# Two more sequences of layer 1 through routed experts, in a two-layer transformer on one core

## The chip, the cores and the metric

The kernel runs on one core of a Trainium2 chip. The metric is the device time of one execution in microseconds. Of the kernel before there are three timed runs and one profiled execution.

## What is computed

Eight sequences of 512 tokens, 128 wide, go through two layers. Each layer is adaptive layer norm, attention with 16 heads of 8, adaptive layer norm again, and a mixture of 8 experts of which each token uses two. Layer 0 has full attention, SwiGLU experts of hidden width 352 and a shared expert; layer 1 has low-rank q, k and v, causal attention and experts with a squared relu. What the change touches is the expert part of layer 1:

```python
def _L1_ffn_ref(x, Wr, W1, W2):           # N = 8 * 512 tokens, E = 8, D = F = 128
    probs = softmax(xf @ Wr)
    w, idx = top_k(probs, 2)
    comb = zeros((N, E)).at[arange(N)[:, None], idx].add(w)
    mid = square(maximum(einsum('nd,edf->enf', xf, W1), 0.0))
    y = einsum('enf,efd->end', mid, W2)
    return einsum('end,ne->nd', y, comb)
```

## The kernel before

The 8 sequences of layer 0 are numbered 0 to 7, the same ones in layer 1 are 8 to 15. The work of a sequence i is cut into steps with names, each on one engine:

- p_*: layer norm (statistics on VectorE, its power on GpSimd, normalisation on ScalarE, a turn on TensorE), projections, and the split of q and k into three bf16 parts that are stored in HBM; "stack" loads them back (tiles QS, KS). "c_ks" writes ones into rows of KS that only the second pass of the scores reads.
- score, rowmax: scores on TensorE and their row maxima on VectorE (line 965), 32 of each; the maxima make a round trip through HBM (max_st, max_ld). Then bscore, expo (ScalarE, line 1320) and pv (line 775).
- u_*, t_*: sums and outputs through HBM and back, division, output projection, residual.
- f_*: layer norm, transposed activations hF, router logits (f_lg, line 1016), top two (f_top, f_idx).

**Two ways through the experts.** A sequence that stands in GROUPS is routed, the others are dense.

*Dense* (`if i not in GROUP`, sequences 10 to 15): all 8 experts on all 512 tokens. For each expert d_up (TensorE, line 873, weights r1), d_relu and d_sq (ScalarE, lines 1395, 1404), d_dn (TensorE, line 880, weights r2), d_y (VectorE times the token's weight, lines 1216, 1223), d_add (GpSimd adds, line 1549); then d_x (lines 1555, 1558) and d_out, the store of the result. Sequences 14 and 15 have four buffers for relu and square, two of which lie in the weight buffers wst of the routed experts; sequence 15 adds up on VectorE.

*Routed* (groups of two sequences, q = 0 to 4): r_hx makes the activations token by token (GpSimd), r_keep keeps the choices, and the rr_* steps (VectorE, lines 1080 to 1151, and two matmuls) count tokens by expert and give each token a place in tiles of 128 that belong to one expert each. r_sc (GpSimd, line 1504) scatters 8 tiles of tokens twice to d_h by indirect DMA. A group has MT = 23 tiles. In layer 1 they go by fours (index L): x_ld loads, x_turn turns (line 828), x_w loads each tile's expert weights by a register, x_up (line 847), relu, square, x_dn (line 865), x_y, and x_st stores to d_y. g_ga (GpSimd, line 1528) gathers 8 tiles twice, g_w weights and adds them (VectorE, lines 1176, 1180), g_x (GpSimd, lines 1536, 1542) adds them into X. In layer 1 the result is then stored.

A scatter waits until the scatter of the tile before in the same half has landed, a gather likewise. The second source tile of the scatters is `r2[:, 0:NT, :]`, so the load of the dense weights r2 (line 264) is put behind the last scatter of the last group.

**What sets the order.** A planner, run when the kernel is built, gives every engine and the SP queue one fixed list. Each step has a weight (its assumed time), a due time ("urgency"), steps it comes after and a lag. Where several steps can start within SLACK of each other on an engine, the one with the smallest due time is put first. The tables SHIFT, LATE, LAST and NUDGE add offsets to due times; NUDGE has one offset for each family and sequence. Waits on semaphores follow from the data; an engine works through its list in order.

## Time and profile before

| | |
|---|---|
| median of three runs | 1128.35 us (1123.76 to 1128.52) |
| profiled execution | 1132.48 us, of which the span is 1130.3 us |
| TensorE matmul busy | 1026.9 us (91%) |
| VectorE busy | 869.8 us (77%) |
| ScalarE busy | 730.9 us (65%) |
| GpSimd busy | 429.5 us (38%) |
| mean granted TensorE clock | 0.949 of full speed |

The page gives busy times over the span, the chain of work that ended last (followed back from the last instruction, at each step to what released it), and the costliest groups of instructions. "x" is a count of instructions; a float32 matmul stands as two passes in the trace, so it counts twice. DVE is VectorE, ACT ScalarE, POOL GpSimd, SP the engine whose queue issues most DMAs. The idle time before an instruction is put down to what ended it.

### The profile page before, as it was taken

To read this page: it belongs to the slowest core of one execution; us is meant where nothing else is said; L and a number is where in the kernel's file an instruction comes from. 1 tells how busy PE (TensorE), PEld (TensorE's weight loads), DVE (VectorE), ACT (ScalarE), POOL (GpSimd) and SP (SyncE) were. 2 spreads that over 40 slices of the span, in tenths; PEclk is the share of its full clock that TensorE was granted. 3 is DMA by queue.
4 is the path that set the end of the run, shared out by engine and by line. 5 is a ranking of instruction groups with operands and counts; after the bars stand their busy time and mean duration, and the time that the engine had idled before them with its cause. 6 is when DMAs were issued, how large, how long until landed. Compare 5 with 4: busy or idle time off the path is not lost.

```text
span 1130.3 us, 22735 instructions
## 1 busy us (share of the span) xinstructions
PE 1026.9 (91%) x8315; PEld 533.1 (47%) x8315; DVE 869.8 (77%) x1814; ACT 730.9 (65%) x1220; POOL 429.5 (38%) x484
## 2 busy tenths in 40 slices
PE   4589999889989999899889999899999889999996
PEld 2112222224555555446555566566565434455464
DVE  3799888898887888797557877777876688687455
ACT  4048766877767776666466566565657767767763
POOL 3000212354033346325135433453344468434463
PEclk9569988999999999999898999999999999999998
DMA  4804434356664777557548577695767846412110
GB/s 136 173 24 129 112 87 114 112 189 180 214 203 149 235 205 215 155 161 201 152 139 230 155 226 232 192 249 179 229 185 220 222 126 183 104 43 61 50 40 19
DMA packets 122510, 176.06 MB, mean 156 GB/s; under 512 B 20280, under 2 KB 86200, under 8 KB 122400
## 3 DMA queue, kind: packets, MB, share of 16 engines
q1 hardware_dynamic: 116064, 161.24, 49.1%
q0 software_dynamic: 5760, 12.59, 3.9%
q8 instruction: 66, 1.08, 0.4%
q10 hardware_dynamic: 576, 0.79, 0.3%
q14 instruction: 44, 0.36, 0.1%
HBM read 114.77 MB, written 59.67 MB: 154 GB/s over the span
## 4 chain that ended last, share of the span: by engine, by line
PE 46%; DVE 20%; DMA 15%; issue 8%; ACT 4%; POOL 3%; SPq 3%; POOLq 0%; DVEq 0%; ACTq 0%
DVE nm L965 12%; PE ps L775 10%; PE ps L837 8%; PE ps L758 5%; PE ps L736 5%; PE ps L856 5%; DMA gr<-d_y,pos 4%; PE ps L873 2%; PE ps L880 2%; DMA DR<-d_r 2%; ACT ES L1320 2%; DMA d_h<-r,pos 2%; PE ps L785 2%; DMA d_r<-DC 1%; PE ps L718 1%
## 5 line engine op out<-in xcount | busy, mean ns | idle before, releaser
L965 DVE TENSOR_REDUCE nm<-ps 128x2 f32<-128x1024 f32 (+3 forms) x512 | 507.7, 1016 | 103.5 <-PE ps L742 57.2
L1320 ACT ACTIVATE ES<-ps 128x1024 f32<-128x1024 f32 (+3 forms) x512 | 430.0, 862 | 160.3 <-PE ps L758 90.1
L775 PE MATMUL ps<-ES,VS 128*9 128x512 f32 (+3 forms) x2048 | 231.1, 528 | 0.8 <-DVE nmp L976 0.4
L736 PE MATMUL ps<-KS,QS 48*128 48x512 bf16 (+3 forms) x1024 | 183.8, 366 | 38.5 <-DVE nm L965 23.6
L758 PE MATMUL ps<-QS,KS 51*128 51x512 bf16 (+3 forms) x1024 | 178.0, 352 | 20.0 <-DVE nm L965 11.6
L837 PE MATMUL ps<-hsT,wst 128*128 128x128 f32 x1104 | 158.6, 288 | 3.7 <-DVE hdx L1158 3.4
L837 PEld LDWEIGHTS ps<-hsT,wst 128*128 128x128 f32 x1104 | 136.9, 194 | 38.6 <-issue 30.1
L758 PEld LDWEIGHTS ps<-QS,KS 51*128 51x128 bf16 x1024 | 49.6, 94 | 173.7 <-DVE nm L965 55.2
L736 PEld LDWEIGHTS ps<-KS,QS 48*128 48x128 bf16 x1024 | 50.0, 95 | 153.6 <-DVE nm L965 59.3
L1528 POOL DMA_INDIRECT gr<-d_y,pos x80 | 83.2, 1040 | 99.4 <-DMA gr<-d_y,pos 63.5
L856 PE MATMUL ps<-wst,hdx 128*128 128x128 f32 x552 | 84.7, 291 | 0.6 <-ACT hsT L1347 0.4
L856 PEld LDWEIGHTS ps<-wst,hdx 128*128 128x128 f32 x552 | 71.4, 197 | 21.5 <-issue 13.2
L1504 POOL DMA_INDIRECT d_h<-hx,pos x40 | 40.0, 999 | 103.5 <-DVE pos L1135 57.7
L1549 POOL TENSOR_TENSOR ya<-ya,yS 128x512 f32<-128x512 f32 x35 | 45.1, 1290 | 73.3 <-DVE yS L1223 73.3
L1456 POOL TENSOR_SCALAR rs<-mv 128x4 f32<-128x4 f32 x32 | 7.5, 236 | 168.2 <-DVE mv L951 167.6
L1158 DVE SCALAR_TENSOR_TENSOR hdx<-tx,ps 128x384 f32<-128x384 f32 x92 | 50.4, 548 | 22.5 <-ACT tx L1353 22.0
L1353 ACT ACTIVATE tx<-ps 128x384 f32<-128x384 f32 x92 | 45.3, 492 | 34.0 <-PE ps L837 32.2
L1259 ACT ACTIVATE xn<-X,rs 128x128 f32<-128x128 f32 x128 | 52.5, 485 | 18.6 <-POOL rs L1461 18.6
L775 PEld LDWEIGHTS ps<-ES,VS 128*9 128x9 f32 x2048 | 31.8, 89 | 68.2 <-issue 53.6
L1465 POOL TENSOR_TENSOR sp<-sr,sp 128x512 bf16<-128x512 f32 x32 | 37.3, 1171 | 56.7 <-ACT sp L1296 56.5
L1165 DVE TENSOR_TENSOR hdx<-ps,hdx 128x384 f32<-128x384 f32 x92 | 50.7, 551 | 9.1 <-PE ps L837 8.2
L742 PE MATMUL ps<-codek,codeq 64*128 64x128 bf16 x512 | 56.3, 219 | 0.0
(196 smaller groups left out, 1405.4 us busy)
## 6 DMA issues: line engine op xcount, KB each, us to landing
wst<-we SPq DMA_DIRECT2D x92, 576.0 KB, 5.1
d_u<-US SPq DMA_DIRECT2D x64, 256.0 KB, 2.7
KS<-d_k SPq DMA_DIRECT2D x64, 192.0 KB, 4.8
QS<-d_q SPq DMA_DIRECT2D x64, 192.0 KB, 5.5
hs<-d_h SPq DMA_DIRECT2D x25, 256.0 KB, 4.0
d_y<-ys SPq DMA_DIRECT2D x25, 256.0 KB, 4.7
d_q<-sp SPq DMA_DIRECT2D x16, 384.0 KB
d_k<-sp SPq DMA_DIRECT2D x16, 384.0 KB, 3.4
```

The source lines that it names most:

```text
L736: mm = eng.matmul(psum[:, bank[u][a], 0:n], QS[m][r:r + KA, pr, 128 * t:128 * t + 128], KS[m][r:r + KA, pr, 0:n], start=True, stop=i < NB)
L742: mm = eng.matmul(psum[:, bank[u][a], n - 128:n], codeq[r:r + 64, :], codek[r:r + 64, :], start=False, stop=True)
L758: mm = eng.matmul(psum[:, bank[u][a], 0:S - q0], KS[m][r:r + KB, pr, 128 * j:128 * j + 128], QS[m][r:r + KB, pr, q0:S], start=True, stop=i ...
L775: mm = eng.matmul(psum[32 * a:32 * a + 9, b, q0:S], VS[i % 3][:, j, 4 * g + a, :], ES[(2 * (NT * (NG * i + g) + j) + a // 2) % NES][:, a % ...
L837: mm = eng.matmul(ps(*u)[:, 128 * n:128 * n + 128], w[:, c, 128 * n:128 * n + 128], hsT[m][:, a0:a0 + 128], start=True, stop=True)
L856: mm = eng.matmul(ps(*u)[:, 0:128], hdx[UNIT[p, j] % 2][:, 128 * n:128 * n + 128], w[:, 2, 128 * n:128 * n + 128], start=(n == 0), stop=(n ...
L965: eng.tensor_reduce(nm[f][:, :].rearrange("p (a c) -> p a c", a=2)[:, :, 4 * pr + t], ps2("score", i, f, pr, t)[:, :, 0:n], AX.X, ALU.max, ...
L1158: eng.scalar_tensor_tensor(out=hdx[m][:, :], in0=tx[m][:, :], scalar=1.0, in1=ps("x_up", p, j, 0)[:, 0:384], op0=ALU.add, op1=ALU.mult).th ...
L1165: eng.tensor_tensor(hdx[m][:, :], ps("x_up", p, j, 1)[:, 0:384], hdx[m][:, :], ALU.mult).then_inc(s[k], 1)
L1259: ins = eng.activation(xn[w][:, t, :], X[:, NT * b + t, :], ACT.Identity, bias=rs[:, w, 2, t:t + 1], scale=rs[:, w, 1, t:t + 1])
L1320: eng.activation(ES[(2 * n + pp) % NES][:, :, 0:S - q0], ps2("bscore", i, f, g, j, pp)[:, :, 0:S - q0], ACT.Exp, scale=SC1 if i >= NB else ...
L1528: eng.indirect_dma_start(out=gr[m][:, :], out_offset=None, in_=d_y[p][:, :], in_offset=bass.IndirectOffsetOnAxis(ap=pos[p % 2][:, c, t8:t8 ...
```

## The change

Sequences 10 and 11 become a sixth group of GROUPS, so they are routed, and only 12 to 15 are dense. Everything sized by GROUPS follows: the group's own indirect DMAs, tiles and waits, r2's load behind the scatters of (10, 2), the dense buffers of sequence 14 behind the last expert of (10, 2). The load of the ones into KS (c_ks) comes after the second stack of sequence 0 in the plan. The assumed times of three counting steps depend on the size of the group; for two sequences they become 0.96, 3.6 and 0.96 us instead of 1.25, 3.8 and 1.2. SLACK goes from 0.05 to 0.15, and all 13 rows of NUDGE are new, by up to some 6 units for the families u, t, g and d.

```diff
--- before.py
+++ after.py
@@ -22,7 +22,7 @@
 
 NST = 4
 
-GROUPS = ((0, 2), (2, 2), (4, 2), (6, 2), (8, 2))
+GROUPS = ((0, 2), (2, 2), (4, 2), (6, 2), (8, 2), (10, 2))
 GMAX = max(n for _, n in GROUPS)
 
 MT = [2 * n * NT + E - 1 for _, n in GROUPS]
@@ -78,19 +78,19 @@
 
 
 NUDGE = {
-    "p": [-0.65, 2.4, 0.46, -0.17, -0.01, 0.52, -0.35, -0.35, -0.36, 0.0, 0.0, 0.0, 0.01, -0.04, 0.06, -0.44],
-    "score": [0.1, 0.0, 0.0, 0.0, 0.0, 0.0, 0.0, 0.0, 0.0, 0.0, 0.0, 0.0, -0.02, 0.03, 0.11, 0.1],
-    "max": [-0.03, 0.04, -0.27, -0.13, -0.32, -0.1, -1.24, -0.14, 0.0, 0.01, 0.0, -0.04, -0.01, 0.28, 0.07, 1.6],
-    "expo": [0.0, 0.0, 0.0, 0.0, 0.0, 0.0, 0.0, 0.0, 0.0, 0.0, -0.04, 0.0, -0.08, -0.02, -0.07, -0.09],
-    "pv": [-0.02, 0.91, 0.27, -0.08, 0.02, -0.01, -0.02, 0.0, 0.0, 0.0, 0.02, -0.01, -0.03, -0.19, -0.25, 0.21],
-    "u": [0.51, -0.26, 0.32, -0.59, -0.7, -0.3, -0.77, -0.67, -0.29, 0.68, 0.99, 0.1, 1.49, 0.61, 0.88, -1.31],
-    "t": [-0.5, -0.89, -0.57, -1.24, -0.7, -1.24, -0.53, -0.05, 0.07, 0.0, 0.01, 0.46, -1.06, 0.77, -0.38, 1.37],
-    "f": [0.01, 0.01, -0.1, 0.01, 0.06, -0.01, 0.0, 0.11, -1.15, -1.33, 0.44, -0.55, -0.34, -1.93, -2.64, -3.12],
-    "s": [0.26, -0.18, 0.01, 0.17, 0.12, -0.09, 0.0, 0.0, 0.0, 0.0, 0.0, 0.0, 0.0, 0.0, 0.0, 0.0],
-    "r": [-0.74, -0.04, 0.02, 0.01, -0.35, -1.37, 0.25, 0.36, 0.45, 1.63, 0.0, 0.0, 0.0, 0.0, 0.0, 0.0],
-    "x": [0.0, 0.0, 0.0, 0.0, -0.64, 0.0, 0.0, 0.0, 0.0, 0.0, 0.0, 0.0, 0.0, 0.0, 0.0, 0.0],
-    "g": [0.52, 1.36, -0.05, 0.59, 0.12, 2.56, 1.49, 0.89, -0.68, 1.19, 0.0, 0.0, 0.0, 0.0, 0.0, 0.0],
-    "d": [0.0, 0.0, 0.0, 0.0, 0.0, 0.0, 0.0, 0.0, -0.48, -1.4, 0.4, 0.18, 0.59, 1.17, 1.02, 0.96],
+    "p": [1.01, 2.21, 0.34, 0.79, 0.04, 1.01, -0.36, -0.36, -0.36, 0.0, 0.0, 0.03, 0.01, -0.07, 0.66, 1.29],
+    "score": [0.09, 0.0, 0.0, 0.0, 0.0, 0.0, 0.0, 0.0, 0.0, 0.0, 0.09, 0.0, -0.05, -0.03, 0.13, 0.08],
+    "max": [-1.47, 0.05, 0.71, -0.45, -1.35, -0.67, -0.64, 0.2, -0.01, 0.08, 0.03, 0.01, 1.32, -1.86, -0.82, -0.21],
+    "expo": [0.0, 0.0, 0.0, 0.0, 0.01, 0.0, 0.0, 0.0, 0.0, 0.0, -0.04, 0.14, 0.06, 0.01, -0.02, 1.08],
+    "pv": [-0.15, 0.94, 0.22, -0.11, -0.01, -0.06, -0.09, -0.03, -0.05, 0.05, 0.07, 0.11, 0.6, 1.55, -0.18, 2.01],
+    "u": [-1.88, -2.81, -0.31, -4.63, -2.38, -5.63, -3.24, -4.06, -1.33, -3.46, -1.45, -1.52, -1.29, -5.93, -5.45, -4.69],
+    "t": [-1.62, -1.87, -0.87, 0.26, -3.41, -2.27, -0.07, 0.12, 0.02, -0.03, -0.35, -1.87, -0.14, 0.03, -0.97, 5.02],
+    "f": [0.17, -1.54, -2.64, 0.09, 0.05, -0.97, 0.05, 0.06, -2.37, -3.46, 0.17, -0.01, -0.59, -0.93, -2.03, -1.12],
+    "s": [0.26, -0.32, 0.02, -0.15, -0.08, -0.09, 0.01, 0.0, 0.0, 0.0, 0.0, 0.0, 0.0, 0.0, 0.0, 0.0],
+    "r": [-1.09, -0.39, -0.04, 0.08, -0.83, -1.16, 0.54, 3.47, 0.62, 0.59, 1.34, 2.9, 0.0, 0.0, 0.0, 0.0],
+    "x": [-0.1, 0.0, 0.0, 0.2, -0.77, 1.19, 0.0, 0.0, 0.0, 0.0, 0.0, 0.0, 0.0, 0.0, 0.0, 0.0],
+    "g": [1.2, 1.31, -1.38, 0.29, -1.94, 2.99, 3.21, 1.03, -5.02, 1.58, -0.45, 4.01, 0.0, 0.0, 0.0, 0.0],
+    "d": [0.0, 0.0, 0.0, 0.0, 0.0, 0.0, 0.0, 0.0, 0.52, -0.61, 0.0, 2.99, 0.34, 1.92, 1.64, 3.53],
 }
 TIED = {"stack": "p", "rowmax": "score", "bscore": "expo", "rr": "r"}
 
@@ -200,7 +200,7 @@
 
 PIPE = 1.3
 WEARLY = 0.2
-SLACK, SWITCH = 0.05, 0.1
+SLACK, SWITCH = 0.15, 0.1
 
 XAT, XLEN = (2.6, 1.6), (2.0, 1.6)
 SPREAD = 2.5, 2
@@ -245,7 +245,7 @@
     add("DVE", ("c_ps",), 3.4, -10.0)
     add("DVE", ("c_one",), 1.2, -1.0, [("m_one", 0)])
     for m in range(NSTK):
-        add("SP", ("c_ks", m), 0.8, 0.1 + 0.1 * m, [("c_one",)], lag=2.5)
+        add("SP", ("c_ks", m), 0.8, 0.1 + 0.1 * m, [("c_one",), ("stack", 0, 1)], lag=2.5)
 
     for b in range(2, NB):
         load(f"x{b}", b - 1.0, 5.0, after=[("stack", b - 1, 1)])
@@ -387,9 +387,9 @@
             u = i + 2.45
             add("DVE", ("rr_oh", q), 0.2, u, [("r_keep", first + c) for c in range(size)])
             add("PE", ("rr_mm", q), 0.4, u, [("rr_oh", q), ("c_more", 1)], opens=1)
-            add("DVE", ("rr_a", q), 1.25, u, [("rr_mm", q)], closes=[("rr_mm", q)])
-            add("DVE", ("rr_pos", q), 3.8, u, [("rr_a", q)] + ([("g_ga", GROUPS[q - 1][0] - 1, t, c) for t in range(NT) for c in range(2)] if q > 1 else []))
-            add("DVE", ("rr_tex", q), 1.2, u, [("rr_pos", q)] + ([("x_reg", q - 2, (MT[q - 2] - 1) // 12)] if q > 1 else []))
+            add("DVE", ("rr_a", q), 0.8 + 0.08 * size, u, [("rr_mm", q)], closes=[("rr_mm", q)])
+            add("DVE", ("rr_pos", q), 3.2 + 0.2 * size, u, [("rr_a", q)] + ([("g_ga", GROUPS[q - 1][0] - 1, t, c) for t in range(NT) for c in range(2)] if q > 1 else []))
+            add("DVE", ("rr_tex", q), 0.7 + 0.13 * size, u, [("rr_pos", q)] + ([("x_reg", q - 2, (MT[q - 2] - 1) // 12)] if q > 1 else []))
             sent = [("rr_pos", q)] * 4
             for t in range(size * NT):
                 for c in range(2):
```

## Rows read from the trace of the kernel before

**Rows 1.** The page's busy times: engine, busy us (share of the span), instructions.

```profile
PE 1026.9 (91%) x8315; PEld 533.1 (47%) x8315; DVE 869.8 (77%) x1814; ACT 730.9 (65%) x1220; POOL 429.5 (38%) x484
```

**Rows 2.** The page's chain that ended last, shares of the span by engine.

```profile
PE 46%; DVE 20%; DMA 15%; issue 8%; ACT 4%; POOL 3%; SPq 3%; POOLq 0%; DVEq 0%; ACTq 0%
```

**Rows 3.** By stretch: busy us (instructions) of PE, PEld, DVE, ACT, POOL; clock; DMA share; GB/s.

```profile
530.00:600.00 70.00, 62.14 (x460) 38.04 (x458) 40.13 (x91) 40.40 (x65) 24.36 (x25) 0.90 0.52 155
870.00:926.00 56.00, 48.14 (x539) 23.40 (x537) 40.22 (x75) 38.36 (x69) 30.72 (x31) 0.97 0.68 191
926.00:1072.00 146.00, 142.05 (x1411) 70.44 (x1407) 106.88 (x251) 109.23 (x193) 71.98 (x70) 1.00 0.33 89
957.00:1124.00 167.00, 158.58 (x1411) 87.53 (x1409) 113.97 (x283) 115.26 (x206) 75.09 (x72) 0.98 0.20 54
```

**Rows 4.** Listing of the dense up line: duration min/median/max, first and last start.

```profile
L873 PE MATMUL ps<-hF,r x80: 592/593/1061, 926.3 to 1102.3; 128*128 128x512 f32 x80
```

**Rows 5.** Groups by shape, TensorE: xcount | busy us, mean ns | idle before, releasers.

```profile
L880 PE MATMUL ps<-r,hd 128*128 128x128 f32 x320 | 44.4, 283 | 0.5 <-DVE sr L958 0.4
...
L873 PE MATMUL ps<-hF,r 128*128 128x512 f32 x80 | 43.9, 647 | 2.2 <-DVE ya L1216 2.2
...
L828 PE MATMUL ps<-ident,hs 128*128 128x128 f32 x115 | 19.2, 290 | 0.1
...
L865 PE MATMUL ps<-wst 128*128 128x128 f32 x46 | 6.7, 288 | 0.0
...
L847 PE MATMUL ps<-hsT,wst 128*128 128x128 f32 x46 | 6.6, 286 | 1.9 <-DMA wst<-wy 1.8
```

**Rows 6.** Groups by shape, ScalarE: the squares of the dense experts.

```profile
L1404 ACT ACTIVATE hd<-tt 128x512 f32<-128x512 f32 x40 | 25.0, 633 | 0.5
```

**Rows 7.** Groups by shape, VectorE, from 870 to 960 us.

```profile
L1180 DVE SCALAR_TENSOR_TENSOR cv<-gr,wts,cv 128x128 f32<-128x128 f32 x16 | 7.8, 489 | 2.6 <-DMA gr<-d_y,pos 2.1
...
L1223 DVE TENSOR_TENSOR yS<-ps,comb 128x512 f32<-128x512 f32 x4 | 2.7, 675 | 0.0
```

**Rows 8.** Groups by shape, GpSimd, whole span.

```profile
L1528 POOL DMA_INDIRECT gr<-d_y,pos x80 | 83.2, 1040 | 99.4 <-DMA gr<-d_y,pos 63.5 <-issue 29.2 <-DMA d_y<-ys 4.4
...
L1549 POOL TENSOR_TENSOR ya<-ya,yS 128x512 f32<-128x512 f32 x35 | 45.1, 1290 | 73.3 <-DVE yS L1223 73.3
...
L1504 POOL DMA_INDIRECT d_h<-hx,pos x40 | 40.0, 999 | 103.5 <-DVE pos L1135 57.7 <-DMA d_h<-hx,pos 38.9 <-issue 6.8
```

**Rows 9.** Timeline of VectorE: start us, us, instruction [idle before].

```profile
800.90 0.19 DVE L1016 TENSOR_TENSOR lg<-lg,sm 128x32 f32<-128x32 f32 x1
...
808.02 0.43 DVE L1080 TENSOR_TENSOR ohb<-ohs 128x64 bf16<-128x64 f32 x1
...
814.79 0.18 DVE L1151 TENSOR_SCALAR tex<-te 128x24 uint32<-128x24 f32 x1
...
944.88 0.19 DVE L1016 TENSOR_TENSOR lg<-lg,sm 128x32 f32<-128x32 f32 x1
```

**Rows 10.** Timeline of GpSimd: scatters, gathers and the last addition of group (8, 2).

```profile
813.80 1.14 POOL L1504 DMA_INDIRECT d_h<-hx,pos  x1 [11.36 <-DVE pos L1135]
...
847.84 0.97 POOL L1504 DMA_INDIRECT d_h<-r,pos  x1 [0.77 <-DMA d_h<-r,pos]
...
909.34 1.01 POOL L1528 DMA_INDIRECT gr<-d_y,pos  x1 [0.35 <-issue]
...
959.86 1.27 POOL L1542 TENSOR_TENSOR X<-X,cv 128x512 f32<-128x512 f32 x1
```

**Rows 11.** Timeline of SP's queue near the start.

```profile
11.35 5.68 SPq L1604 DMA_DIRECT2D KS<-wst  x8
```

**Rows 12.** The chain that ended last, its pieces near the start: start us, us, what.

```profile
16.97 1.53 ACT xn L1259 x4
...
56.06 16.98 DVE nm L965 x15
```

**Rows 13.** DMA issues: KB each, median us from issue to landing.

```profile
r<-wr SPq DMA_DIRECT2D x2, 512.0 KB, 3.9
```

## The prediction

> **What bounds the kernel now.** I read the page first: TensorE is busy for 1026.9 of 1130.3 us [rows 1], and it holds 46% of the chain that ended last, with VectorE at 20% and DMAs at 15% [rows 2]. A share that high over the whole span still hides stages, so the busy times by stretch come next [rows 3]. The reader should see three kinds. From 926 to 1072 us dense expert work of layer 1, whose first matmul starts at 926.3 [rows 4], lies beside attention: TensorE is busy for 142.05 of 146 us, 0.973. From 870 to 926 us no dense work exists yet, only attention and the routed end of sequences 6 to 9: 48.14 of 56 us, 0.86, and its granted clock slips to 0.97. From 530 to 600 us, around the change of layers, 62.14 of 70. So where dense work is on offer TensorE is the limit, and where it isn't TensorE waits for attention's round trips. Then the groups of instructions by engine gave prices [rows 5 to 8], and the timelines gave the latency of the one layer 1 group that is routed already, sequences 8 and 9 [rows 9, 10].
>
> **What goes and what comes on TensorE.** The dense block of a sequence is 8 products up (16 passes in the trace) and 32 down (64 passes). The five sequences 10 to 14 spend 43.9 and 44.4 us on them [rows 5], so one costs 8.8 + 8.9 = 17.7 us, and two that go save 35.3. In their place comes what group (8, 2) has: 23 tiles turned (19.2 us for the five groups, 3.8 for one), 23 up (46 passes, 6.6 us), 23 down (6.7 us), and two small counting matmuls; the dearest small matmul shown has a mean of 0.290 us, so 0.6 at most [rows 5]. That is 17.7 us. TensorE is relieved of 35.3 - 17.7 = 17.6 us.
>
> **The other engines.** ScalarE loses 16 relus and 16 squares, 32 x 0.633 = 20.3 us with the row of the squares for both, and gets four passes over 23 tiles, 5.75 full banks each, 23 x 0.633 = 14.6 us [rows 6]: 5.7 us less. VectorE loses 16 products at 0.675, 10.8 us, and gets 8 pairs of weighting at 0.489 each, 7.8 us, beside the counting chain, which fills 808.0 to 814.9 us for the present group between other work; some 4.6 us of it are its own, an estimate from 20 short instructions of 0.17 to 0.46 us. It comes out within 2 us of even [rows 7, 9]. GpSimd loses 14 additions at 1.29 and two closing pairs at 1.27 each half, 23.1 us, and gets 16 scatters at 1.0, 16 gathers at 1.04, and four full-tile pairs at 1.27 each half (two masks, two closings), 10.2 us: 42.8 us, so +20 us busy [rows 8, 10]. It has room: 75.09 of 167 us from 957 on [rows 3]. But it also stands still for its own transfers: before 80 gathers it was idle for 99.4 us, 1.24 each, so 16 take 36 us of its queue if nothing is put between them [rows 8].
>
> **When the new group can run.** Its router needs sequence 11, whose logits are ready at 944.88 us; for sequence 9 that was 800.90 [rows 9]. From 800.90 the present group needs 12.9 us to the first scatter (813.80), 34.0 more to the last one's issue (847.84), 61.5 to its first gather (909.34), and 51.8 to the end of its last addition into X (959.86 + 1.27): 160.2 us [rows 10]. Laid from 944.88: scatters 958 to 993, gathers from 1053, done at 1105, and some 5 us for the store of the result, an estimate a little above that load's time: 1110. The dense block of sequence 12 now has to wait as well. Its second weights (r2) share memory with the second scatter source and are loaded behind the last scatter, now 993 instead of 849; with the 3.9 us that such a load takes to land, 997 [rows 13]. The third and fourth buffers of sequences 14 and 15 come free with the group's last expert, about 1050; that costs nothing unless TensorE gets to the block of 14, the last but one, before then.
>
> **The sum.** From 926 to 997 us, 71 us, the dense work that filled TensorE is gone and nothing can take its place. I give this stretch the share of its neighbour before it, 0.86 for 0.973: 71 x 0.113 = 8.0 us of the saving stay unused [rows 3]. Attention's round trips (maxima out and back, sums out and back) are what ends last there. Behind 997 dense work of 12 to 15 (71 us) and the experts (17.7) fill it as now. Net 17.6 - 8.0 = 9.6 us: span 1130.3 - 9.6 = 1120.7. The routed chain's 1110 lies before that by 10 us. The profiled execution took 1132.48 (2.2 beside its span) and the median of the runs shown is 1128.35, 4.1 below, so 1128.35 - 9.6 = 1118.7, say 1118.5.
>
> **The small edits.** The ones for KS hold SP's queue from 11.35 to 17.03 us [rows 11] ahead of the first stores. Moved behind the first stacks they free it, but the chain there runs through ScalarE (normalisation of sequence 1, 16.97 to 18.50, ahead of the second part of the split) [rows 12], and the stack waits for the third part. Gain 0 to 1.6 us; I take 0. Behind the stacks the eight issues (5.7 us) stand before sequence 1's stores, whose scores come only after the maxima of sequence 0, the last of which end at 73.0 us [rows 12]: 0, or 5.7 us if that cover went. The smaller weights of the three counting steps, the slack and the offsets execute nothing; they change orders on all five queues over the whole span. The trace has no row for that. I bound it by the hole at 530 to 600: at 0.973 it would be 68.1 busy for 62.14, so 6 us to gain and, as a second hole like it, 6 to lose; I take 0 since no row leans either way.
>
> **A rule against this change.** Indirect DMAs are what the change adds on GpSimd. Over 80 scatters and 80 gathers the trace shows means of 1.0 and 1.04 us, beside a VectorE that is three quarters busy [rows 3, 8]. The Trainium skill, page "SBUF — State Buffer", section "SBUF: two separate sides", says that while VectorE copies or scales in its two-port mode GpSimd cannot write a transfer's descriptors, and that such a DMA of some 0.62 us alone took about 3.1. Estimated by that page, 32 new ones would hold GpSimd 99 us in place of 33, which would make it the limit. The trace doesn't show it, so it gets no chance beyond that of rival (b), whose price is made from rows and which it would bring about.
>
> **Rivals.** (a) *The saving is swallowed by the gap.* If dense work of 12 can't start at 997 (its logits or the order on the queues hold it) and TensorE runs at 0.86 over all 146 us from 926 to 1072, 146 x 0.113 = 16.5 us are lost, net 1.1: 1127. For it: the dense block is the only filler, and sequence 12's own attention must be through. Against: attention, freed of 35 us of competing matmuls, gets there sooner.
> (b) *GpSimd's queue puts the routed chain last: slower.* GpSimd works in order. The dense additions of 12, 13 and 14 (7 x 1.29 + 2 x 1.27 = 11.6 us each, 35) now share the time from 993 to 1105 with scatters, gathers and their waits. If all of them fall in series with the routed chain, it ends at 1110 + 35 = 1145, 14.7 us over the present span: 1143. For it: while the present group's scatters ran, no dense block had begun [rows 4, 10]. It decides from the point where more than 11 of the 35 us are in series (1120.7 - 1110); if 20 are, it is level with now. Against it: waits of 1.24 us before a gather can take an addition of 1.29.
> (c) *No gap at all.* Reordered attention fills TensorE without dense work: -17.6, and with the hole at 530 closed -23.6: 1110.8 to 1104.8. Against it: the routed chain's 1110 on the span's scale (1106 on the median's) is a floor unless sequence 11's logits come sooner.
> (d) *The offsets do the most,* in either direction, by up to 6 us and for reasons apart from the routing; it widens each case.
>
> **How the numbers follow.** Forecast, 1112 to 1122.7: 0.46. (c), below 1112: 0.13. (a) and weak forms of (b), within 0.5% (1122.7 to 1134): 0.23. (b) beyond: 0.18. Half a per cent is about what a measurement of this kernel can tell from no change. So faster 0.59, same 0.23, slower 0.18. Range 1105 to 1138: it takes in most of (c) and the nearer part of (b).
>
> **What would show it.** TensorE's busy time falls by 17 to 18 us; the share between 926 and the last scatter is about 0.86, with the granted clock slipping for moments; the last scatter is issued near 993 and dense matmuls down start just after it; the last addition of sequence 11 is 10 us or more before the end, with sequence 15's dense block last as now. Wrong: if scatters or gathers stand last in the chain (b); if TensorE's share stays at 0.86 past 1010 (a); if the time moved before 870 us (d).

## The result, with the profile after

The changed kernel is slower, by 1.2%. Its median is 1140.68 us (1134.48 to 1144.05, four runs) beside 1127.55 us for the kernel before on the same chip (1123.76 to 1128.52, four runs): a ratio of 1.0116 with an interval of 1.0067 to 1.0166. Measured again on two other chips the ratio was 1.0078 (1.0050 to 1.0105) and 1.0153 (1.0095 to 1.0211). The prediction said 1118.5 and a range of 1105 to 1138, so the time lies outside, on the side that was given 0.18. Five executions of all that follow stand out as slow and are left out of the ratios, though not of the medians: three of the kernel before, one of run 3, and one of run 10 (2602.78 us). The profiled execution took 1140.92 us with a span of 1139.1, 8.8 more than the span before.

The busy times of the page, changed kernel; they answer to [rows 1]:

```profile
PE 1028.0 (90%) x8272; PEld 532.0 (47%) x8272; DVE 880.2 (77%) x1832; ACT 726.7 (64%) x1212; POOL 450.8 (40%) x506
```

TensorE has 43 instructions fewer, and yet 1.1 us more busy time, where 17.6 less were forecast. The instructions themselves are not the cause. The groups of TensorE by shape, changed kernel (count, busy us, mean ns, idle before), stand against [rows 5]:

```profile
L873 PE MATMUL ps<-hF,r 128*128 128x512 f32 x48 | 28.1, 685 | 3.1 <-DVE ya L1216 2.2 <-DVE yS L1223 0.6 <-DVE lg L1016 0.2
L880 PE MATMUL ps<-r,hd 128*128 128x128 f32 x192 | 26.1, 280 | 2.8 <-DVE yT L995 1.7 <-DVE yS L1223 1.1
L828 PE MATMUL ps<-ident,hs 128*128 128x128 f32 x138 | 22.1, 281 | 0.7 <-DMA hs<-d_h 0.6
L865 PE MATMUL ps<-wst 128*128 128x128 f32 x92 | 14.4, 302 | 0.0
L847 PE MATMUL ps<-hsT,wst 128*128 128x128 f32 x92 | 13.2, 285 | 0.2 <-ACT ES L1320 0.2
```

The dense groups fall by 15.8 and 18.3 us, the three routed ones rise by 2.9, 7.7 and 6.6: 16.9 us net of the 17.6 worked out. All other matmuls together take 18.0 us more, with the same work. Where that happens is seen in the busy times by stretch, changed kernel, in the columns of [rows 3]:

```profile
530.00:600.00 70.00, 67.11 (x547) 40.90 (x545) 48.75 (x101) 47.23 (x75) 27.61 (x28) 0.98 0.64 187
870.00:926.00 56.00, 48.67 (x483) 24.61 (x481) 35.24 (x77) 36.64 (x66) 32.13 (x34) 0.88 0.55 160
926.00:1072.00 146.00, 131.87 (x1285) 64.27 (x1286) 100.05 (x243) 99.47 (x178) 82.57 (x83) 0.89 0.51 145
957.00:1124.00 167.00, 153.59 (x1356) 83.86 (x1351) 106.73 (x264) 111.60 (x202) 89.75 (x89) 0.94 0.37 106
...
926.00:1000.00 74.00, 62.81 (x621) 27.55 (x621) 56.57 (x150) 47.49 (x86) 47.70 (x49) 0.82 0.62 170
```

The same last stretch of the kernel before:

```profile
926.00:1000.00 74.00, 70.95 (x700) 34.77 (x696) 57.56 (x127) 56.55 (x100) 44.99 (x46) 1.00 0.50 128
```

From 926 to 1000 us TensorE's share is 62.81 / 74 = 0.849 for 0.959, and the granted clock has a mean of 0.82 of full speed for 1.00. The clock has two levels, 1.2 and 2.4 GHz, so 0.82 means 2 x 0.18 x 74 = 27 us at 1.2 GHz there, and 0.88 from 870 to 926 another 13: 40 us for 3.4 before. It fell while TensorE worked in pieces with waits between them. What that does to a matmul, in the groups by shape from 870 to 996 us, changed kernel first, then the kernel before:

```profile
L775 PE MATMUL ps<-ES,VS 128*9 128x512 f32 x80 | 13.5, 753 | 0.1
```

```profile
L775 PE MATMUL ps<-ES,VS 128*9 128x512 f32 x80 | 10.8, 610 | 0.2
```

The same 80 matmuls take a mean of 753 ns for 610. So the busy time that was saved came back as slower matmuls, 1.1 us more than was saved, and the idle time of TensorE grew from 103.4 to 111.1 us: 1.1 + 7.7 = 8.8, the growth of the span. This is how the account closes, not yet what the cause is.

The new group itself. GpSimd's timeline, changed kernel (start, us, instruction, idle before in brackets): first and last scatter, first gather, last addition into X.

```profile
948.53 1.16 POOL L1504 DMA_INDIRECT d_h<-hx,pos  x1 [1.93 <-DVE pos L1135]
...
984.18 0.98 POOL L1504 DMA_INDIRECT d_h<-r,pos  x1 [0.30 <-issue]
...
1034.73 1.17 POOL L1528 DMA_INDIRECT gr<-d_y,pos  x1 [7.85 <-issue]
...
1080.51 1.27 POOL L1542 TENSOR_TENSOR X<-X,cv 128x512 f32<-128x512 f32 x1
```

It is done at 1081.8, 57 us ahead of the end. Two listings of the changed kernel (duration min/median/max, first and last start) show when dense work begins, the first line answering to [rows 4]:

```profile
L873 PE MATMUL ps<-hF,r x48: 592/595/1220, 1031.8 to 1113.6; 128*128 128x512 f32 x48
```

```profile
L865 PE MATMUL ps<-wst x92: 275/275/581, 869.0 to 1030.9; 128*128 128x128 f32 x92
```

The first dense matmul starts at 1031.8, right behind the last product of the last routed expert at 1030.9, and not at 997.

Last, VectorE's timeline gives the moments at which a sequence's router logits are ready, here of sequences 11 to 15 in the changed kernel and then in the kernel before, whose first is the 944.88 of [rows 9]:

```profile
932.50 0.19 DVE L1016 TENSOR_TENSOR lg<-lg,sm 128x32 f32<-128x32 f32 x1
990.29 0.19 DVE L1016 TENSOR_TENSOR lg<-lg,sm 128x32 f32<-128x32 f32 x1
1032.43 0.19 DVE L1016 TENSOR_TENSOR lg<-lg,sm 128x32 f32<-128x32 f32 x1
1091.33 1.04 DVE L1016 TENSOR_TENSOR lg<-lg,sm 128x32 f32<-128x32 f32 x1
1113.70 0.19 DVE L1016 TENSOR_TENSOR lg<-lg,sm 128x32 f32<-128x32 f32 x1
```

```profile
1001.51 0.19 DVE L1016 TENSOR_TENSOR lg<-lg,sm 128x32 f32<-128x32 f32 x1
1048.05 0.19 DVE L1016 TENSOR_TENSOR lg<-lg,sm 128x32 f32<-128x32 f32 x1
1080.28 0.86 DVE L1016 TENSOR_TENSOR lg<-lg,sm 128x32 f32<-128x32 f32 x1
1102.46 0.19 DVE L1016 TENSOR_TENSOR lg<-lg,sm 128x32 f32<-128x32 f32 x1
```

Sequences 11, 12 and 13 are 12.4, 11.2 and 15.6 us ahead of before; sequences 14 and 15 are 11.1 and 11.2 behind. The lead is there and is lost between 13 and 14.

The traces narrow down where. The exponentials (expo, line 1320) go through the sequences one after another. Their listing for sequences 14 and 15 together (duration min/median/max, first and last start), changed kernel and then before:

```profile
L1320 ACT ACTIVATE ES<-ps x64: 366/712/1032, 976.3 to 1079.9; 128x1024 f32<-128x1024 f32 x16, 128x768 f32<-128x768 f32 x16, 128x512 f32<-128x512 f32 x16, 128x256 f32<-128x256 f32 x16
```

```profile
L1320 ACT ACTIVATE ES<-ps x64: 378/730/1032, 981.1 to 1072.1; 128x1024 f32<-128x1024 f32 x16, 128x768 f32<-128x768 f32 x16, 128x512 f32<-128x512 f32 x16, 128x256 f32<-128x256 f32 x16
```

The changed kernel begins them 4.8 us ahead and ends them 7.8 us behind: 103.6 us for 91.0. What follows lasts 59.2 us for 58.2, so nearly the whole growth of the span is there once they are through. Two more traces of the changed kernel have 104.9 and 100.0 us (runs 9 and 12 below). In this stretch, from 976 to 1080 us, stand the new group's expert products, 17.1 us of TensorE, and 14.1 us of its passes on ScalarE.

Sequence 14 is sequence 6 in layer 1 and can't start ahead of the routed result of 6 in layer 0. GpSimd's timeline, the addition that closes one half of it, changed kernel and then before:

```profile
896.42 1.27 POOL L1542 TENSOR_TENSOR X<-X,cv 128x512 f32<-128x512 f32 x1
```

```profile
893.72 1.27 POOL L1542 TENSOR_TENSOR X<-X,cv 128x512 f32<-128x512 f32 x1
```

That is 2.7 us later, in a kernel whose TensorE has been relieved of work that lay behind this point.

### The profile page after: what moved, and what is told of

It reads as the page before. It is cut to its first block, busy times and chain, and to the rows that moved or that the text cites. A ratio compares the mean times of both kernels' runs of the same rounds, so it can differ in the third digit from the quotient of the medians.

```text
span 1139.1 us, 22772 instructions
## 1 busy us (share of the span) xinstructions
PE 1028.0 (90%) x8272; PEld 532.0 (47%) x8272; DVE 880.2 (77%) x1832; ACT 726.7 (64%) x1212; POOL 450.8 (40%) x506
## 4 chain that ended last, share of the span: by engine, by line
PE 38%; DVE 18%; DMA 17%; issue 12%; POOL 8%; ACT 5%; SPq 1%; POOLq 0%; DVEq 0%; ACTq 0%
DVE nm L965 9%; PE ps L775 9%; PE ps L837 6%; PE ps L758 5%; DMA gr<-d_y,pos 5%; DMA d_h<-hx,pos 4%; PE ps L736 4%; DMA d_h<-r,pos 4%; PE ps L856 3%; ACT ES L1320 3%; PE ps L803 2%; DMA DR<-d_r 2%; POOL d_h L1504 1%; PE ps L718 1%; DMA d_r<-DC 1%
## 5 line engine op out<-in xcount | busy, mean ns | idle before, releaser
L775 PE MATMUL ps<-ES,VS 128*9 128x512 f32 (+3 forms) x2048 | 236.0, 537 | 0.9 <-ACT VS L1303 0.3
L736 PE MATMUL ps<-KS,QS 48*128 48x512 bf16 (+3 forms) x1024 | 187.2, 371 | 34.1 <-DVE nm L965 19.9
L758 PE MATMUL ps<-QS,KS 51*128 51x512 bf16 (+3 forms) x1024 | 182.8, 360 | 22.0 <-DVE nm L965 14.6
L1528 POOL DMA_INDIRECT gr<-d_y,pos x96 | 100.5, 1046 | 134.2 <-DMA gr<-d_y,pos 60.6
L1504 POOL DMA_INDIRECT d_h<-hx,pos x48 | 48.1, 1003 | 110.8 <-DVE pos L1135 55.4
L1504 POOL DMA_INDIRECT d_h<-r,pos x48 | 47.4, 987 | 55.8 <-DMA d_h<-r,pos 35.3
L1377 ACT ACTIVATE ys<-ps 128x128 f32<-128x128 f32 (+1 forms) x104 | 32.6, 313 | 45.4 <-PE ps L856 38.0
L763 PE MATMUL ps<-codeq,codek 64*128 64x128 bf16 x512 | 57.8, 227 | 0.0
```

The costliest lines, as they stand in the source:

```text
L736: mm = eng.matmul(psum[:, bank[u][a], 0:n], QS[m][r:r + KA, pr, 128 * t:128 * t + 128], KS[m][r:r + KA, pr, 0:n], start=True, stop=i < NB)
L758: mm = eng.matmul(psum[:, bank[u][a], 0:S - q0], KS[m][r:r + KB, pr, 128 * j:128 * j + 128], QS[m][r:r + KB, pr, q0:S], start=True, stop=i ...
L763: mm = eng.matmul(psum[:, bank[u][a], 0:128], codek[r:r + 64, :], codeq[r:r + 64, :], start=False, stop=True)
L775: mm = eng.matmul(psum[32 * a:32 * a + 9, b, q0:S], VS[i % 3][:, j, 4 * g + a, :], ES[(2 * (NT * (NG * i + g) + j) + a // 2) % NES][:, a % ...
L1504: eng.indirect_dma_start(out=d_h[:, :], out_offset=bass.IndirectOffsetOnAxis(ap=pos[p % 2][:, c, t8:t8 + 1], axis=0), in_=hx[t8 // NT][:, ...
L1528: eng.indirect_dma_start(out=gr[m][:, :], out_offset=None, in_=d_y[p][:, :], in_offset=bass.IndirectOffsetOnAxis(ap=pos[p % 2][:, c, t8:t8 ...
```

## The experiments

Each was run beside the kernel before on the same chip; its medians there were 1129.0 to 1130.5 us. Ratios are to it, with the 95% interval. Runs 1 to 4 shared a chip, so did 5 to 8, 9 to 11, 12 to 15, and 16 to 18; the number of a run is that in its name. In runs 1, 3, 6, 7, 8, 10, 17 and 18 the time came out above every range that was written down beforehand.

**Is it the routing or the rest of the diff?** Runs 1 and 2 take one of the two alone.

```diff
--- before.py
+++ e1_groups_only
-GROUPS = ((0, 2), (2, 2), (4, 2), (6, 2), (8, 2))
+GROUPS = ((0, 2), (2, 2), (4, 2), (6, 2), (8, 2), (10, 2))
```

> The kernel before with the sixth group (10, 2) alone: old due-time offsets, slack, place of the ones and step weights. Theory T (tail): the last group's experts stand ahead of all dense work in TensorE's order, so from about 926 us to the last expert matmul at 1031 nothing fills TensorE, it idles in pieces and spends about 41 us at 1.2 GHz where before it spent 3; that comes with the group, so this kernel is slower than before by at least as much as the changed one, 1138 to 1150 us. Theory O (offsets): the routing saves its 17 us of TensorE work and the new offsets lose more: 1112 to 1124 us.

```diff
--- after.py
+++ e2_edits_only
-GROUPS = ((0, 2), (2, 2), (4, 2), (6, 2), (8, 2), (10, 2))
+GROUPS = ((0, 2), (2, 2), (4, 2), (6, 2), (8, 2))
```

> The changed kernel with the old five groups: new offsets, slack, step weights and place of the ones, but sequences 10 and 11 dense. T: dense work fills TensorE from 926 us again, the clock stays at 2.4 GHz there, and the time is near before, 1122 to 1134 us (offsets made for another grouping may cost some). O: the loss comes from the offsets, so 1138 us or more with the loss before 870 us.

Measured: the group alone 1160.73 us, 1.0246 (1.0187 to 1.0305); the edits alone 1151.06, 1.0160 (1.0097 to 1.0222). So +31.6 and +21.9 us, and both together +13.1. The two don't add up: each alone is worse than both. Run 2's loss isn't ahead of 870 us, as the expectation had it: the logits of 10 come at 860.5 us (860.9 before) and those of 11 at 928.9, 16.0 us ahead; those of 12 are 6.3 ahead and those of 13, at 1057.9, 9.9 behind. A lead is lost late there too, with no sixth group. Whether the offsets or the slack cost in run 2 is taken up with run 18.

**Are dense products that wait for the last expert the cause?** Line 456 of the planner lists, for each dense product up, what its bank must wait for, the last routed expert among it. Run 3 keeps that only where memory demands it.

```diff
--- after.py
+++ e3_dense_free
-                old = [("s_dn", NB - 1), ("s_gate", NB - 1, 0), ("s_gate", NB - 1, 1), ("x_dn",) + UNITS[-1]]
+                old = [("s_dn", NB - 1), ("s_gate", NB - 1, 0), ("s_gate", NB - 1, 1)] + ([("x_dn",) + UNITS[-1]] if i >= N - 2 else [])
```

> The changed kernel, with the planner's rule that every dense matmul up stands behind the last routed expert kept for sequences 14 and 15 alone (12 and 13 use no buffer of the experts). T: the dense block of 12 starts when its weights r2 are in, 990 to 1000 us instead of 1032, fills part of the gap, and the kernel gains 6 to 12 us on the changed one: 1128 to 1135 us. O, and the theory G that GpSimd's queue of gathers sets the end: no gain, 1138 to 1143 us.

Measured: 1150.78 us, 1.0179 (1.0130 to 1.0228). The first dense matmul now starts at 988.5, 43 us sooner, in the listing of that run:

```profile
L873 PE MATMUL ps<-hF,r x48: 592/592/748, 988.5 to 1110.8; 128*128 128x512 f32 x48
```

Its profiled execution, the fastest of its six, had a span of 1140.1, about that of the changed kernel, and the median is not better. A dense block that starts sooner bought nothing here. The new plan moves other steps too, so this doesn't price the late start by itself.

**Does the clock carry the loss?** Two matmuls of 128 columns ahead of every second score step of sequences 13 and 14 (64 of them, some 18 us by the price of the dense ones, 23.5 us busy in run 15 and 21.8 in run 5) fill TensorE where it waits. Runs 4 and 15 put them into the changed kernel, run 5 into the kernel before, whose clock is at 1.00 there.

```diff
--- after.py
+++ e4_warm_after
+                    if i in (13, 14) and t % 2 == 0:
+                        for c in range(2):
+                            eng.matmul(psum[:, bank[u][0], 128 * c:128 * c + 128], ident[:, :], ident[:, :], start=True, stop=True)
```

> The changed kernel with 64 extra 128x128x128 float32 matmuls on the identity, 2 ahead of every second score step of sequences 13 and 14 (into the bank that the step then overwrites); the order is otherwise untouched. By the dense down rows they cost 64 x 0.28 = 18 us of TensorE at full clock, as much as the change took away. Theory C (clock): they keep the clock at 2.4 GHz between 870 and 1005 us, the same attention matmuls get their old durations back (615 for 753 ns in the longest), and the time grows by less than 6 us, or falls: 1136 to 1146 us. If the clock is a side effect without weight: the time grows by 12 to 18 us, 1152 to 1158 us.

> The kernel before with the same 64 extra float32 matmuls on the identity ahead of score steps of sequences 13 and 14. Its clock is at 2.4 GHz there already, so it has nothing to win back: by 64 x 0.28 = 18 us of TensorE its time grows by 12 to 18 us (1140 to 1146 us). In the changed kernel the same matmuls cost 11 us (1151.6 for 1140.7). Theory C (the clock carries part of the loss) wants this growth to be larger than 11 us, by 4 or more; if it is 11 or less, the clock has no weight in the time.

> The 64 warming matmuls (18 us by their price) in the changed kernel, against the changed kernel of this call; in the kernel before they cost 10 us (1139.2 for 1129.0). If the clock carries part of the loss they cost clearly less here, at most 6 us; if it doesn't, 8 to 12 us.

Measured: run 4 1151.58 us, 1.0174 (1.0118 to 1.0229); run 5 1139.22, 1.0090 (1.0064 to 1.0116), 10.2 over the kernel before; run 15 1154.03 beside 1144.56 for the changed kernel on its chip, 9.5 more. The stretches of run 15 show that the fill does what it should to the clock, 1.00 and 0.91 for 0.88 and 0.82:

```profile
870.00:926.00 56.00, 53.23 (x554) 31.21 (x553) 35.74 (x77) 38.17 (x69) 32.88 (x36) 1.00 0.56 159
926.00:1000.00 74.00, 62.90 (x620) 30.33 (x620) 54.23 (x123) 41.71 (x74) 47.66 (x49) 0.91 0.49 141
```

Had the low clock set the time, the fill should have cost less where it lifts the clock than where nothing is to be lifted. It cost the same, 9.5 and 10.2. But by the intervals of runs 12 and 15 the 9.5 is good to some 9 us either way, so a clock worth a few us isn't ruled out here; run 10 below is the stronger evidence. No return from lifting the clock is seen.

**Is it the group's own chain, or the dense block of 12?** Runs 6 and 13 leave the 16 new gathers out, run 14 most of the products of sequence 12's dense block; run 12 is the changed kernel itself beside 13 to 15.

```diff
--- after.py
+++ e6_no_gather
...
+                    if i in (10, 11):
+                        continue
```

> The changed kernel, same order, with the 16 gathers of group (10, 2) left out (sequences 10 and 11 get stale rows; only the wait for the stored tiles is kept). Theory G (GpSimd in order: gathers between 1035 and 1075 us hold dense additions, the closing of sequence 12 and with it the gates of 14) expects 6 to 14 us less than the changed kernel, 1127 to 1135 us. Theory T (TensorE's gap and clock ahead of 1031 us, and the dense work that is late by it) expects at most 4 us: 1137 to 1142 us.

> The changed kernel once more, as the measure for the three variants of this call, since a variant without the gathers had come out at 1149 us on another chip, behind by 9 us already ahead of the place where it differs. 1136 to 1150 us; whatever it is, the variants are read against it.

> The 16 gathers of group (10, 2) left out, read against the changed kernel of this call. Theory G (gathers hold GpSimd and with it the closing of sequence 12): 6 to 14 us below it. Theory T (lost filler, clock, late dense work): at most 4 us below it.

```diff
--- after.py
+++ e14_thin12
-                    eng.matmul(ps(*u), r1[:, e, :], hFs[i], start=True, stop=True).then_inc(s["d_up"], 1)
+                    w = 64 if i in (12,) else S
+                    eng.matmul(ps(*u)[:, 0:w], r1[:, e, :], hFs[i][:, 0:w], start=True, stop=True).then_inc(s["d_up"], 1)
...
-                    for t in range(NT):
+                    for t in range(1 if i in (12,) else NT):
```

> The changed kernel with the dense experts of sequence 12 cut on TensorE to 64 of 512 columns up and 1 of 4 tiles down (this part of the result is left out), 14.4 us of matmuls between 1031 and 1063 us. If dense work that starts late makes TensorE the limit of the tail, this buys 8 to 14 us against the changed kernel of this call. If the latency of the last attention or GpSimd sets the tail, under 4 us.

Measured: run 6 1149.34 us, 1.0185 (1.0156 to 1.0214), on a chip without the changed kernel; run 12 1144.56, 1.0153 (1.0095 to 1.0211); run 13 1146.74, 1.0134 (1.0055 to 1.0213); run 14 1149.37, 1.0187 (1.0104 to 1.0270). Neither taking the gathers away nor taking the dense products of 12 away makes the changed kernel faster: runs 13 and 14 are 2.2 and 4.8 us above run 12, within the noise. Rival (b) needs the gathers and falls; that dense work of 12 short of room costs time, as rival (a) has it, is not seen either.

**Is it the wait for the gates of 14?** The gates of sequence 14 are loaded into a buffer that sequence 12 must have left. Run 7 gives a third buffer to the changed kernel, run 17 to the kernel before.

```diff
--- after.py
+++ e7_gt3
-        GT = [sb(f"GT{i}", [128, 4, 128]) for i in range(2)]
+        GT = [sb(f"GT{i}", [128, 4, 128]) for i in range(3)]
...
-        GTs = [GT[i % 2][:, :, :] if i < N - 1 else fs[:, 0:S].rearrange("p (k f) -> p k f", k=4) for i in range(N)]
+        GTs = [GT[i % 3][:, :, :] if i < N - 1 else fs[:, 0:S].rearrange("p (k f) -> p k f", k=4) for i in range(N)]
```

> The changed kernel with a third buffer for the gates, so that the gates of 14 wait for sequence 11 and not for the closing of 12 (1068 us in the changed kernel, with the residual of 14 at 1076). If this wait sets the end: 6 to 10 us less, 1131 to 1135 us, with the logits of 14 near 1060 to 1075 in place of 1091. If sequence 15's attention and TensorE's remaining work set it: within 4 us of 1140.7, though the logits of 14 come sooner.

> The kernel before with a third buffer for the gates, so that the gates of 14 need not wait for the closing of 12 (logits of 14 at 1080 us, 35 us after its attention output; they should come by 1065). If that late wait costs time at the end: 1120 to 1126 us, better than both kernels. If the chain of sequence 15 sets the end, as in the changed kernel where the third buffer brought the logits of 14 forward by 17 us for nothing: 1126 to 1134 us.

Measured: run 7 1150.17 us, 1.0166 (1.0132 to 1.0200); run 17 1138.87, 1.0088 (1.0057 to 1.0120). In run 7 the logits of 14 came at 1074, 17 us sooner than in the changed kernel, and those of 15 at 1127, 13 later. Both kernels came out slower with one wait less: the planner orders the steps anew around it, and in run 7 what 14 gained, 15 lost.

**What is the order worth?** Run 8 is the changed kernel with the offsets of before, run 18 the kernel before with one number of the planner changed, run 11 the kernel before with only the ones moved. Run 9 is the changed kernel once more.

```diff
--- after.py
+++ e8_old_offsets
...
-    "score": [0.09, 0.0, 0.0, 0.0, 0.0, 0.0, 0.0, 0.0, 0.0, 0.0, 0.09, 0.0, -0.05, -0.03, 0.13, 0.08],
+    "score": [0.1, 0.0, 0.0, 0.0, 0.0, 0.0, 0.0, 0.0, 0.0, 0.0, 0.0, 0.0, -0.02, 0.03, 0.11, 0.1],
...
```

> The changed kernel with the table of offsets of before; slack, place of the ones, step weights and the sixth group as changed. The group alone gave 1160.7 us. If the new table is what won 20 us back: 1155 to 1165 us. If slack, ones or weights did: 1138 to 1148 us.

```diff
--- before.py
+++ e18_slack_only
-SLACK, SWITCH = 0.05, 0.1
+SLACK, SWITCH = 0.15, 0.1
```

> The kernel before with SLACK 0.15 in place of 0.05 and nothing else: the same instructions, in lists that differ where steps can start within 0.15 of each other. Theory L expects this alone to move the time by more than 6 us, the bound that the prediction gave to all offsets together: 1135 to 1150 us. If orders weigh little: 1125 to 1134 us.

```diff
--- before.py
+++ e11_ones_only
-        add("SP", ("c_ks", m), 0.8, 0.1 + 0.1 * m, [("c_one",)], lag=2.5)
+        add("SP", ("c_ks", m), 0.8, 0.1 + 0.1 * m, [("c_one",), ("stack", 0, 1)], lag=2.5)
```

> The kernel before with the ones for KS behind the first stacks and nothing else. In the changed kernel the first scores start at 30 us instead of 34. The prediction said 0 to 1.6 us of gain. If the first loads gain 3 us and the rest follows: 1123 to 1127 us; if later waits take it up: within 2 us of before.

> The changed kernel itself once more, beside the runs of before of this call. Its four runs so far lie between 1134.5 and 1144.1 us, while six variants of it lie near 1150. If the variants really lose, it stays at 1138 to 1144 us. If its time simply spreads from call to call, 1145 to 1152 us.

Measured: run 8 1177.11 us, 1.0449 (1.0384 to 1.0514); run 18 1178.25, 1.0436 (1.0375 to 1.0497); run 11 1129.53, 0.9998 (0.9964 to 1.0032); run 9 1137.99, 1.0078 (1.0050 to 1.0105). Run 18 executes exactly the instructions of the kernel before, in another order, and takes 49 us more. It loses them over the whole middle of the kernel. The busy times from 600 to 870 us, run 18 and then the kernel before:

```profile
600.00:870.00 270.00, 249.40 (x2409) 158.32 (x2408) 196.71 (x446) 153.91 (x296) 109.81 (x118) 0.97 0.66 196
```

```profile
600.00:870.00 270.00, 261.04 (x2588) 167.94 (x2584) 204.85 (x490) 167.84 (x327) 114.47 (x124) 0.99 0.71 210
```

All engines do less there, VectorE and ScalarE too (446 and 296 instructions for 490 and 327), as they would if they waited for each other. With the sixth group and the new slack, the new offsets are worth 1177.11 - 1129.0 = 48.1 less 13.1, that is 35 us. On five groups they are worth some 27 us beside the new slack: run 18 with the old offsets is +49.1, run 2 with the new ones (and the ones and weights) +21.9. So the new offsets don't fit six groups alone, and the slack is the likelier cost in run 2; the new offsets with the old slack were not run.

Read by groups, the same runs show that the routing has no price of its own. With the old order it costs 31.6 us (run 1). With the new slack and the old offsets it costs nothing that can be seen, 1178.25 us with five groups and 1177.11 with six (runs 18 and 8, the latter with the new place of the ones and the new weights as well). With all the edits in place it brings +21.9 us down to +13.1, 8.8 less by the medians; the ratios, 1.0160 and 1.0116, lie within each other's intervals, so this gain is not clear of noise.

**Is a relief of TensorE worth its busy time at all?** Run 10 takes dense products away from the kernel before and touches nothing else: same lists, same waits, same transfers.

```diff
--- before.py
+++ e10_thin_dense
-                    eng.matmul(ps(*u), r1[:, e, :], hFs[i], start=True, stop=True).then_inc(s["d_up"], 1)
+                    w = 64 if i in (10, 11) else S
+                    eng.matmul(ps(*u)[:, 0:w], r1[:, e, :], hFs[i][:, 0:w], start=True, stop=True).then_inc(s["d_up"], 1)
...
-                    for t in range(NT):
+                    for t in range(1 if i in (10, 11) else NT):
```

> The kernel before, same order, with the dense experts of sequences 10 and 11 cut on TensorE: 64 of 512 columns up, 1 of 4 token tiles down (this part of the result is left out; every other step and wait stays). That takes about 2 x (8.8 x 7/8 + 8.9 x 3/4) = 29 us of matmuls away and adds nothing. The prediction took the relief at its full price but for 8 us of gap: then 19 to 23 us less, 1105 to 1109 us. Theory T (without this work TensorE cannot be filled, and its clock falls) expects less than half: 1114 to 1127 us, with granted clock below 0.95 between 926 and 1020 us.

Measured: 1129.01 us over 10 executions, 1.0005 (0.9974 to 1.0037). By columns 29 us of matmuls are gone. The groups by shape of run 10 show it as less, since a pass of 64 columns still has a mean of 302 ns:

```profile
L881 PE MATMUL ps<-r,hd 128*128 128x128 f32 x224 | 34.9, 291 | 0.9 <-DVE yS L1224 0.6
L874 PE MATMUL ps<-hF,r 128*128 128x512 f32 x48 | 24.9, 617 | 2.2 <-DVE ya L1217 2.2
...
L874 PE MATMUL ps<-hF,r 128*128 128x64 f32 x32 | 6.7, 302 | 0.0
```

That is 66.5 us for the 88.3 of [rows 5], 21.8 less, more than the change was to save. The page of run 10:

```profile
PE 1017.5 (90%) x8219; PEld 524.7 (47%) x8219; DVE 869.0 (77%) x1814; ACT 729.7 (65%) x1220; POOL 429.7 (38%) x484
```

Of the 21.8 only 9.4 are seen in TensorE's busy time (4.9 beside the 1022.4 of run 11, which is the kernel before but for the ones), and none in the median: the interval leaves room for a gain of 3 us. The rest of the 21.8 went into slower matmuls at a lower clock; but not even what TensorE was less busy by reached the end. Its stretch from 926 to 1000 us:

```profile
926.00:1000.00 74.00, 65.61 (x625) 29.97 (x625) 59.23 (x134) 54.39 (x100) 42.84 (x45) 0.86 0.49 127
```

Share 0.887 and clock 0.86, in a kernel that has no sixth group and the old offsets: the picture that the changed kernel shows, and at no cost. So the thin stretch with its low clock is what a relieved TensorE looks like here, and TensorE's work in it did not set the time.

**And with the group's work away?** Run 16 keeps the changed kernel's lists and leaves out the work of the sixth group.

```diff
--- after.py
+++ e16_no_group
...
-                    for t in range(n):
+                    for t in range(1 if p == 5 else n):
...
+                    if p == 5:
+                        continue
...
```

> The changed kernel, same lists, with the work of group (10, 2) left out: no scatters, no gathers, one tile of four on TensorE in its experts (8 us of matmuls gone), so sequences 10 and 11 get no experts at all. Theory A (the added group's work is what costs): it falls to the time of before or below, 1115 to 1130 us. Theory L (what costs is the lists: what stands behind what on each engine, with attention's round trips setting the pace): it stays above 1134 us.

Measured: 1134.32 us over 10 executions, 1.0049 (1.0016 to 1.0083). That is a hair above the 1134 of theory L. The changed lists still don't reach the kernel before when they carry neither the dense products of sequences 10 and 11 nor the new group's scatters, gathers and most of its TensorE products. Its loads, its passes on ScalarE and its weighting on VectorE stay, so this run doesn't tell their cost from that of the order. With the work left out here the kernel takes 4 us more (by run 9, whose interval overlaps this one) to 10 us more (by run 12), both on other chips. The exponentials of 14 and 15 take 95.3 us in run 16, between the 91.0 of before and the 103.6 of the changed kernel. So of the loss of 8 to 15 us some 5 are left with less work, and the rest goes with the group's own work, though not clear of the noise by every pair.

## Why the prediction was wrong, step by step

**What bounds the kernel.** Here is the first step that failed. The text took 0.973 busy from 926 to 1072 us to mean that TensorE is the limit there, so that each microsecond taken from it would be gained but for a gap. Run 10 took 21.8 us of dense matmuls out of the same blocks and gained nothing, with an interval of some 0.3% to either side. In part the other matmuls grew slower, and for the rest the dense ones fill time in which TensorE would wait anyway. What it waits for is not tested; the traces suggest attention's round trips, and the layer 0 results from which sequences 14 and 15 start. A warning was at hand: [rows 2] gives TensorE 46% of the chain, not 91%.

**TensorE's relief, 17.6 us.** The count was right to the instruction (160 passes go, 115 and two come: 43 fewer) and the sum nearly (16.9). What it is worth was not: nothing in run 10, for 17.6 less a gap.

**The gap, 8.0 us.** Its share was right, 0.849 against 0.86, and the text said that the clock would slip for moments. It slipped for 40 us, which made the other matmuls 18.0 us longer; the sum held no term for that. Whether it needed one is doubtful: run 10 has a low clock too (0.86 from 926 to 1000 us) without a loss, and runs 4, 5 and 15 see no return from lifting it, within their noise.

**The other engines.** GpSimd +21.3 us (20 forecast) and ScalarE -4.2 (5.7 forecast) were right. VectorE, within 2 of even by the text, gained 10.4; the instructions that stretch beside GpSimd (last section) are part of it.

**The new group's timeline.** From the logits of 11 to the first scatter 16.0 us (12.9 forecast), to the last one 35.7 more (34.0), to the first gather 50.5 (61.5), to the end of the last addition 47.1 (51.8): each step held within some 11 us, and the chain ended at 1082 instead of 1105.

**Dense work from 997 us.** Wrong by 35 us. The text looked at the load of r2 alone and missed line 456, by which every product up is ordered behind the last routed expert. Run 3, which lifts that rule for 12 and 13, is no faster, though its lists differ elsewhere too.

**The small edits.** The ones were put at 0 and measured 0 (run 11). Slack and offsets were bounded by 6 us either way, from a hole at 530 us that has nothing to do with an order. That bound was the second failed step, and by its size the larger: the slack alone is +49, the offsets win 35 of it back beside the group, and all the edits without the group are +22 for a term of 0. Taken in this order, edits first, the miss is this term alone, for the group then takes 8.8 off, next to the 9.6 forecast. That agreement is luck: with the group first it is +31.6. The hole at 530 was closed, by the way (67.11 for 62.14), and the 5 us that this looked worth are not to be seen in the time.

**Rivals.** (a) had its condition right: the order held the dense work of 12 back, to 1031.8 us. Its mechanism wasn't there: from 996 to 1032 us TensorE was busy for 35.68 of 36 us, with the new group's experts among the rest, its share from 926 to 1072 was 0.903 and not 0.86, and runs 3 and 14 found no price on dense 12. (b) gave a time near the measured one, 1143, by a mechanism that wasn't there: the routed chain ends 57 us early, and without its gathers the kernel isn't faster (runs 6, 13). (c) is out by its time. (d) named a right place, with a bound eight times too small for the slack alone (49 for 6).

**What stays open.** Which places in the lists cost the 8 to 15 us. The loss is seen while the exponentials of 14 and 15 run, 12.6 us longer than before, where the new group's experts stand between them; that these are the cause is argued from run 16 alone. Sequence 14 also starts its maxima 4 us later than before. Single suspects (the gates' buffer, dense 12, the gathers, the clock) each showed no gain when taken away. Runs 3, 7 and 17 also reorder everything, so they can't clear their suspects alone. No version beat the kernel before.

## What to carry to other kernels

A share of 0.97 on one engine doesn't price its work: before counting removed instructions as time, thin them in place (same lists, same waits, less to compute) and see whether the end moves at all. Where a planner makes in-order lists, every change to what it plans is also a change of order, and its price has to be bounded by a run with the same work in another order, not by a hole in the trace; here it was 49 us, five times the effect looked for. And take slack, offsets and grouping as one: the group without the other edits, the edits without the group, and the group with the new slack but the old offsets were all worse than either kernel.

## What the runs showed of the hardware

**The granted clock fell where TensorE worked in pieces.** From 926 to 1000 us, with waits between the pieces, its mean was 0.82 (changed kernel) and 0.86 (run 10) for 1.00, and the pv matmuls of 128x512 took 753 ns for 610 between 870 and 996 us. The Trainium skill, page "TensorE: Matmul & The Clock Gate", section "HAM oscillation — how this bites in real kernels", says that a TensorE which waits between bursts is throttled again and starts each burst cold. The trace agrees in that the clock was lower where the waits lay; single bursts were not looked at. With such a clock busy time is no measure of work: 43 instructions fewer came out as 1.1 us more, and between profiles of one kernel the busy time differs by 7 us (1028.0 here, 1021.0 in run 12), more than the small terms of the sum.

**VectorE is stretched beside GpSimd.** A scaling of 128x128 took 1.86 us, five times its mean of 374 ns in the kernel before, while GpSimd ran an addition from 1051.40 to 1052.68. VectorE's timeline, changed kernel:

```profile
1050.90 1.86 DVE L1176 TENSOR_SCALAR cv<-gr,wts 128x128 f32<-128x128 f32 x1
1052.80 0.35 DVE L1180 SCALAR_TENSOR_TENSOR cv<-gr,wts,cv 128x128 f32<-128x128 f32 x1
```

Of the 48 scalings of this line five took over 0.6 us (1.13 to 1.86), and each of the five overlapped a tensor operation on GpSimd; the 41 that overlapped none took 0.46 at most. The mean over the 48 is 425 ns. The indirect DMAs themselves were not held up: 96 gathers have a mean of 1.05 us and 96 scatters 1.0, as before. The rule of the Trainium skill that the prediction weighed (page "SBUF — State Buffer", section "SBUF: two separate sides", some 3.1 us for such a DMA beside a copying VectorE) is not seen in this kernel, where the longest gather or scatter took 1.43 us. The scalings here are short, so the rule is tested weakly; for this kernel the rows decide.
